# First attention of a two-layer block: max subtraction as four 32x64 products, preparation in 32-column strips with the keys one step ahead, reciprocals widened on GpSimd

## The chip, the core and the metric

One core of a Trainium2 chip. The metric is the device time of one execution in microseconds. The profiler records one execution; its span runs from the first to the last instruction, and the device time has a part outside it. PE is TensorE (matmuls; its weight loads are shown apart as PEld), DVE is VectorE, ACT is ScalarE, POOL is GpSimd, SP is SyncE.

## The reference

An input x of 128 sequences x 64 tokens x 128 channels goes through two layers, each a cross attention to a context (128 x 64 x 96) and a mixture of experts, each added to x with a tanh gate. The change touches the first attention alone:

```
xn = (x - mean(x)) / sqrt(var(x) + 1e-5)
q = xn @ wq + bq ; k = ctx @ wk + bk ; v = ctx @ wv + bv        # 16 heads of 8 channels
attn = softmax(q k^T / sqrt(8))                                 # per head, 64 x 64
x = x + tanh(g_xattn[0]) * ((attn v) @ wo + bo)
```

The rest (a mixture of 6 experts, the second attention with one head of 128, a mixture of 8 experts of which each token uses two) follows, and its code is not changed.

## The kernel before

x is held on chip as 64 tiles of 128 tokens (two sequences each). Four tiles make a group; there are 16 groups. The first attention is a software pipeline of steps: step t works on tile t for the scores, t-1 for the exponential, t-2 for the sums and the transposes of the probabilities, t-3 for the product with the values and t-4 for the output product. Within a group the steps are u0 to u3 (`u % GT`). The loop body holds eight steps, two groups. Every engine runs its own list of work in order, written out by hand in its `step`; semaphores join the lists. No planner sets the order.

On PE, a step runs: scores (L663, 32 rows x 64 columns of the array, with the head's keys spread so that four heads share one product), the subtraction of the row maxima from scores already in PSUM (L673, a product of the transposed maxima with a 0/1 matrix of head columns, added to the bank), in u0 the keys' preparation for the next group (L638), the output product (L686), the first half of the transposed probabilities (L690), the transpose of the widened reciprocals (L706), the product with the values (L719, 128 x 32 tiles), the preparation listed for the step in `PREP_AT` (u0: transposed rows L633, u1: queries L638, u2: values L644, u3: none), the second half of the transposes (L690), and the transpose of the maxima (L737).

ACT takes the exponential (L571), copies each PSUM bank out (L578 probabilities, L591 raw heads, L602 maxima, L542/L547/L554/L561 preparation), and normalises the rows of the group after next (L534, one tile in u1, one in u2, two in u3).

DVE makes the sums (L409), the maxima (L412), the reciprocals of the sums (L418), the maxima in two bf16 parts (L423, L425), the reciprocals widened from 16 heads to 128 channels (L430), the addition to x (L436), the product of raw heads and transposed reciprocals (L443), in u0 the layer norm's statistics of the group after next (L375, L379), in u1 its offset (L385), in u2 half the copy of the values (L393).

POOL's work has three parts per group. In u0 it makes the inverse deviation of the group after next (L70, L72) from DVE's statistics. In u1 it spreads the next group's keys into four zero-padded copies, one per head of a set of four (L494), and then adds the output bias to the group after next's x (L485), which waits for ACT's last normalisation of those rows, at the end of u3. In u2 and u3 it has nothing of its own.

PSUM has one bank for all four preparations (`prep`), so each waits for the copies of the one before. SP loads x and the context of a group once the values of the group two before are prepared. Two buffers alternate for scores, probabilities, spread keys and widened reciprocals; the narrow reciprocals have one.

Of the kernel before, what the change touches and what calls it, by code (L numbers as in the profile page):

```python
# [44 lines left out]
def static(t):  # L45
    return isinstance(t, int)
# [233 lines left out]
def attention_of_layer0(nc, sb, psum, sem, c, a, X, dispatch):  # L280
# [21 lines left out]
    denom = sb("a_denom", [P, H], F32)  # L302
    rec = sb("a_rec", [P, H], F32)
    wide_rec = [sb(f"a_wide_rec{i}", [P, H, DH], F32) for i in range(2)]
# [25 lines left out]
    KEYS, ROWS, QUERIES, VALUES = range(PREP)  # L330
    PREP_AT = ((ROWS,), (QUERIES,), (VALUES,), ())
    NORMALISE_AT = ((), (0,), (1,), (2, 3))
    LAST = TILES + 4

# [13 lines left out]
    def group_at(g0, more):  # L348

        return None if static(g0) and g0 + more >= G else g0 + more  # L350

    with nc.Block() as block:
# [16 lines left out]
        def _(dve):  # L369
# [26 lines left out]
            def step(t, u, g0):  # L396
# [17 lines left out]
                if m is not None:  # L414
                    dve.wait_ge(sum_done, m + 1)
                    if not static(m) or m >= 1:
                        dve.wait_ge(wide_rec_ready, m)
                    dve.reciprocal(rec[:], denom[:]).then_inc(rec_done, 1)  # L418
                if n is not None:
# [5 lines left out]
                    dve.tensor_tensor(max_parts[:, :, 1], max_by_bank, max_parts[:, :, 0], ALU.subtract).then_inc(parts_ready, 1)  # L425
                if m is not None:
                    if not static(m) or m >= 2:
                        dve.wait_ge(spread_mm, m - 1)
                    dve.wait_ge(rec_done, m + 1)
                    dve.tensor_copy(wide_rec[u % 2][:], rec[:].unsqueeze(2).broadcast_to([P, H, DH])).then_inc(wide_rec_ready, 1)  # L430
                w = tile_now(t, 4)
# [43 lines left out]
        @block.gpsimd  # L475
        def _(pool):
            def deviation(g):

                wait_alone(pool, stats_done, g + 1)
                inverse_deviation(pool, stats[:], c.minus_half[:], rstd[:], rstd_step, g)  # L480

            def add_bias(g):

                wait_alone(pool, xn_ready, g + 1)
                pool.tensor_tensor(X[:, bass.ts(g, GT), :], X[:, bass.ts(g, GT), :],  # L485
                                   c.out_bias0[:].unsqueeze(1).broadcast_to([P, GT, D]), ALU.add).then_inc(bias_added, 1)

            def spread_k(g, par):

                wait_alone(pool, prep_ev, PREP * g + KEYS + 1)  # L490
                if not static(g) or g >= 2:
                    wait_alone(pool, scores_mm, GT * (g - 1))
                for j in range(4):
                    last = pool.tensor_scalar(keys_of_head(par, j), kT[:],  # L494
                                              c.head_of_group[:, j:j + 1], None, ALU.mult)
                last.then_inc(k_heads_ready, 1)

            def step(t, u, g0):
                if u % GT == 0:
                    g = group_at(g0, 2)  # L500
                    if g is not None:
                        deviation(g)
                if u % GT == 1:
                    g = group_at(g0, 1)
                    if g is not None:
                        spread_k(g, (u // GT + 1) % 2)
                    g = group_at(g0, 2)
                    if g is not None:
                        add_bias(g)

            pool.memset(c.parts[:], 0.0)
            pool.memset(c.minus_half[:], -0.5).then_inc(c.zeroed, 1)
            pool.memset(c.v_heads[0][:].rearrange("p b u w -> p (b u w)"), 0.0).then_inc(c.zeroed, 1)
            wait_alone(pool, c.zeroed, 1)
            deviation(0)
            pool.memset(c.v_heads[1][:].rearrange("p b u w -> p (b u w)"), 0.0).then_inc(c.zeroed, 1)
            deviation(1)
            wait_alone(pool, c.out_bias_done, 1)
            add_bias(0)
            add_bias(1)  # L520
            loop_steps(pool, 2 * GT, TILES // (2 * GT) - 2, LAST, step)
            later_zeros(pool, c, dispatch)
            c.ln.deviation(pool, 0)
            c.ln.offset(pool, 0)

        @block.scalar
        def _(act):
# [36 lines left out]
            def step(t, u, g0):  # L564
# [15 lines left out]

                g = group_at(g0, 1)
                if u % GT == 0 and g is not None:
                    evacuate(g, (u // GT + 1) % 2, KEYS)
                if tile_now(t, 2) is not None:
                    keep_transposed(t - 2, 0)
                n = tile_now(t, 3)
                if n is not None:
# [3 lines left out]
                    act.copy(heads_raw[:], pv[:, 0]).then_inc(raw_ready, 1)  # L591
                g = group_at(g0, 1)
                if g is not None:
                    for k in PREP_AT[u % GT]:
                        evacuate(g, (u // GT + 1) % 2, k)
                if tile_now(t, 2) is not None:
# [25 lines left out]
        def _(pe):  # L622
            def prepare(g, par, k):
# [10 lines left out]
                if k in (KEYS, QUERIES):  # L634
                    w, src = (c.wk0, ctxT[par]) if k == KEYS else (c.wq0, xnT)
                    for h in range(2):
                        for odd in range(2):
                            last = pe.matmul(prep[S * odd:S * odd + S, bass.ts(h, GW // 2)], w[:, bass.ts(h, D // 2)],  # L638
                                             src[:].rearrange("p (t b q) -> p b t q", b=2, q=S)[:, odd],
                                             start=True, stop=True)  # L640
                if k == VALUES:
                    for b in range(GB):
                        for odd in range(2):
                            last = pe.matmul(prep[S * odd:S * odd + S, bass.ts(b, D // 2)], ctxT[par][:, bass.ts(b, S)],  # L644
                                             c.wv0[:].rearrange("p (u h w) -> p h u w", h=2, w=DH)[:, odd],
                                             start=True, stop=True)
                last.then_inc(prep_mm, 1)

            def step(t, u, g0):
# [19 lines left out]
                if n is not None:  # L669

                    pe.wait_ge(rows_ready, n + 1)
                    for s in range(2):
                        last = pe.matmul(scores[(u + 1) % 2][:, s, :], rows[bass.ts(s, STRIP), :], c.head_cols[bass.ts(s, STRIP), :],  # L673
                                         start=False, stop=True, skip_group_check=True)
                    last.then_inc(sub_mm, 1)
                g = group_at(g0, 1)
                if u % GT == 0 and g is not None:
                    prepare(g, (u // GT + 1) % 2, KEYS)
                n = tile_now(t, 4)
# [21 lines left out]
                if n is not None:  # L701
# [20 lines left out]
                    last.then_inc(pv_mm, 1)  # L722
                g = group_at(g0, 1)
                if g is not None:
                    for k in PREP_AT[u % GT]:
                        prepare(g, (u // GT + 1) % 2, k)
                n = tile_now(t, 2)
# [1287 lines left out]
```

## Time and profile before

| | |
|---|---|
| median of three runs | 916.31 us (911.5 to 917.06) |
| profiled execution | span 826.4 us; no total of its own is recorded |
| the runs' median less that span | 89.9 us |
| PE busy, share of the span | 91% |
| PEld | 71% |
| DVE | 83% |
| ACT | 69% |
| POOL | 57% |
| mean granted TensorE clock | 0.972 of full speed |

Busy shares are averages over the whole span, and the stages have different limits; the first attention fills the span from about 20 to 320 us. A matmul's busy time counts it from issue to a modelled end, and matmuls overlap, so a busy PE is not PE at its peak. In a timeline, several instructions of one line stand together as one row with their count, and the time in brackets is the idle time of that engine before the row, with what ended it. "Issue" there is time in which the engine waited for nothing that the profile shows.

### The profile page before, as it was taken

The page shows a single profiled execution, that of the slowest core. Times are in us where ns is not written, and L with a number is a line of the kernel's source. Part 1 is how long each engine was busy: PE and PEld are TensorE (multiplying, and loading weights), DVE is VectorE, ACT ScalarE, POOL GpSimd, SP SyncE. Part 2 cuts the span into 40 slices and gives each one's busy share as a digit, 9 for nine tenths or more (in the row PEclk, how much of TensorE's full clock was granted, in tenths as well). Part 3 has the DMA queues.
Part 4 walks back from the last instruction along what each step waited for, and adds up shares of the span by engine and source line. Part 5 has one row for each costly group of instructions (what it writes and reads, how often), then busy time and mean ns, then how long its engine had stood idle before and what let it go on. Part 6 is the DMA issues. An engine that isn't in the chain of part 4 may idle for free. (4 is left out here: it accounts for less than half of the span.)

```text
span 826.4 us, 26460 instructions
## 1 busy us (share of the span) xinstructions
PE 755.1 (91%) x8408; PEld 584.3 (71%) x8408; DVE 687.7 (83%) x2993; ACT 571.1 (69%) x1209; POOL 472.0 (57%) x504
## 2 busy tenths in 40 slices
PE   3899999999999997999999999998799999999970
PEld 2566666666666654667767767766699999999960
DVE  3889898988989896878888888977589888889965
ACT  2777777777777765688888898855566666666630
POOL 3445554444455601225777777776577777777770
PEclk9999999999999997999999999989999999999995
DMA  9200001000000002001111111113233443346838
GB/s 241 64 25 26 23 22 42 25 22 22 22 22 22 2 2 66 1 11 33 49 44 54 50 43 56 48 51 94 56 84 99 113 110 101 100 124 201 232 99 305
DMA packets 62212, 57.96 MB, mean 70 GB/s; under 512 B 10320, under 2 KB 52099, under 8 KB 62115
## 3 DMA queue, kind: packets, MB, share of 16 engines
q1 hardware_dynamic: 44547, 34.25, 15.3%
q0 software_dynamic: 8640, 17.84, 6.3%
q10 hardware_dynamic: 8928, 4.70, 2.0%
q8 instruction: 45, 0.74, 0.4%
q14 instruction: 52, 0.43, 0.2%
HBM read 32.74 MB, written 24.02 MB: 69 GB/s over the span
## 5 line engine op out<-in xcount | busy, mean ns | idle before, releaser
L1131 POOL DMA_INDIRECT contributions<-v_heads,d_token x142 | 141.6, 997 | 43.3 <-issue 25.3
L1115 POOL DMA_INDIRECT sorted_rows<-r_send,r_slots x128 | 126.5, 988 | 44.7 <-issue 42.0
L1860 PE MATMUL bc_bank<-d_xT,d_w 128*128 128x128 f32 x1136 | 151.7, 277 | 0.1
L1860 PEld LDWEIGHTS bc_bank<-d_xT,d_w 128*128 128x128 f32 x1136 | 139.0, 193 | 0.5 <-DVE d_xT L1377 0.4
L1636 ACT ACTIVATE b_hidden<-bc_bank 128x256 f32<-128x256 f32 x142 | 54.5, 384 | 72.5 <-PE bc_bank L1860 71.9
L494 POOL TENSOR_SCALAR a_k_heads<-a_kT,first 128x512 f32<-128x512 f32 x60 | 93.1, 1570 | 0.8 <-ACT a_kT L547 0.8
L1630 ACT COPY d_w<-w 128x512 f32 x142 | 87.1, 614 | 8.1 <-issue 6.0
L571 ACT ACTIVATE a_probs<-a_scores 128x1024 f32<-128x1024 f32 x64 | 65.6, 1025 | 29.4 <-PE a_scores L673 29.3
L412 DVE TENSOR_REDUCE a_neg_max<-a_scores 128x16 f32<-128x1024 f32 x64 | 78.1, 1221 | 8.1 <-PE a_scores L663 6.5
L578 ACT COPY a_probsT<-a_probsT_bank 128x512 f32<-128x512 f32 x128 | 74.8, 584 | 13.7 <-PE a_probsT_bank L690 13.2
L690 PE MATMUL a_probsT_bank<-first,a_probs 128*128 128x128 f32 x512 | 80.2, 279 | 2.2 <-ACT a_probsT L578 0.3
L409 DVE TENSOR_REDUCE a_denom<-a_probs 128x16 f32<-128x1024 f32 x64 | 77.3, 1209 | 1.7 <-issue 1.3
L663 PE MATMUL a_scores<-a_k_heads,a_qT 32*64 32x256 f32 x1024 | 70.8, 391 | 2.9 <-issue 2.8
L485 POOL TENSOR_TENSOR X<-X,out_bias 128x512 f32 (+1 forms) x16 | 20.3, 1271 | 87.5 <-ACT a_xn L534 84.9
L690 PEld LDWEIGHTS a_probsT_bank<-first,a_probs 128*128 128x128 f32 x512 | 57.9, 142 | 12.5 <-issue 6.0
L1705 PE MATMUL bc_bank<-b_xnT,w 128*128 128x512 f32 x96 | 50.2, 636 | 0.1
L1388 DVE TENSOR_SCALAR v_heads<-bc_bank,d_ends 128x128 f32<-128x128 f32 x142 | 48.7, 343 | 0.5 <-PE bc_bank L1879 0.5
L1756 PE MATMUL bc_bank<-w,b_weighted 128*128 128x128 f32 x384 | 46.8, 278 | 0.0
L663 PEld LDWEIGHTS a_scores<-a_k_heads,a_qT 32*64 32x64 f32 x1024 | 33.1, 132 | 19.3 <-issue 9.3
L1879 PE MATMUL bc_bank<-w_in,b_hidden 128*128 128x128 f32 x288 | 44.7, 278 | 0.5 <-DVE v_heads L1388 0.5
L1372 DVE TENSOR_TENSOR b_hidden<-b_hidden,bc_bank 128x256 f32<-128x256 f32 x72 | 30.1, 418 | 17.8 <-PE bc_bank L1879 10.5
L1756 PEld LDWEIGHTS bc_bank<-w,b_weighted 128*128 128x128 f32 x384 | 44.1, 192 | 0.4
(212 smaller groups left out, 1870.1 us busy)
## 6 DMA issues: line engine op xcount, KB each, us to landing
d_rows<-sorted_rows SPq DMA_DIRECT2D x142, 65.0 KB
X<-in_x SPq DMA_DIRECT2D x16, 256.0 KB, 3.0
b_hidden<-contributions SPq DMA_DIRECT2D x8, 512.0 KB
b_weighted<-contributions SPq DMA_DIRECT2D x8, 512.0 KB, 5.8
out_x<-X ACTq DMA_DIRECT2D x16, 256.0 KB
ctxT<-in_ctx_T SPq DMA_DIRECT2D x16, 192.0 KB, 2.9
c_ctxT<-in_ctx_T SPq DMA_DIRECT2D x16, 192.0 KB, 2.4
contributions<-v_heads,d_token POOLq DMA_INDIRECT x142
```

Source lines behind the costliest of these rows:

```text
L409: dve.reduce_sum(denom[:], probs[u % 2][:].rearrange("p (h k) -> p h k", k=S), AX_X).then_inc(sum_done, 1)
L412: dve.tensor_reduce(neg_max[:], scores[u % 2][:].rearrange("p a (h k) -> p (a h) k", k=S), AX_X, ALU.max, negate=True).then_inc(max_done, 1)
L494: last = pool.tensor_scalar(keys_of_head(par, j), kT[:], c.head_of_group[:, j:j + 1], None, ALU.mult)
L571: act.activation(probs[(u + 1) % 2][:], scores[(u + 1) % 2][:].rearrange("p a n -> p (a n)"), ACT.Exp, scale=SCALE0).then_inc(exp_done, 1)
L578: act.copy(probsT[u % 2][:, half * HU // 2:(half + 1) * HU // 2, :].rearrange("p u q -> p (u q)"), probsT_bank[:]).then_inc(pT_ev, 1)
L663: last = pe.matmul(scores[u % 2][S * b:S * b + S, s, bass.ts(h, 4 * S)], qT[par][rows_in, h, tile, :], k_heads[par][rows_in, tile, h].rear ...
L690: last = pe.transpose(probsT_bank[:, bass.ts(k, P)], probs[u % 2][:, bass.ts(half * HU // 2 + k, P)], c.ident[:])
L1115: pool.indirect_dma_start(dispatch.rows, bass.IndirectOffsetOnAxis(ap=slots[n % 2][:, k, j:j + 1], axis=0), send[n % 2][k][:, j, :], None) ...
L1131: pool.indirect_dma_start(dispatch.contributions, bass.IndirectOffsetOnAxis(ap=token[:, t % KEEP:t % KEEP + 1], axis=0), shares[t % KEEP], ...
L1630: act.copy(w12[t % 3][:], c.w12[:, bass.ds(experts[t % 4], 1)].rearrange("d a i h -> d (a i h)")).then_inc(w12_ready, 1)
L1756: last = pe.matmul(y[:, bass.ts(j, P)], weighted[n % 2][:, k, bass.ts(j, P)], c.w2_0[:, k, :], start=(k == 0), stop=(k == C0 - 1))
L1860: last = pe.matmul(uv[m % 2][:, bass.ts(i, P)], w12[m % 3][:, bass.ts(i, P)], xT[m % 4][:], start=True, stop=True)
```

## The change

The change has four parts, all in the first attention.

- The subtraction of the maxima (L673) is written as four products of 32 rows x 64 columns, one for each bank and half of the tokens, where it was two of 32 x 128.
- Keys, queries and values are prepared by products of 32 weight columns (128 x 32 tiles, the shape of L719) where they were of 64; there are twice as many products on as many streamed columns each.
- The keys' preparation and its copies by ACT move from u0 to u3 of the group before (PE: after the product with the values; ACT: after the raw heads), so the keys of a group are prepared one step earlier. The keys of group 1 are done in step 0.
- The widening of the reciprocals moves from DVE to POOL, first in POOL's step, for tile t-3; the narrow reciprocals get a second buffer. POOL's spreading of keys is divided over the steps (head 0 in u0 after the deviation, heads 1 and 2 in u1, head 3 in u2), the bias addition moves from u1 to u3, and the zero-filling for later stages from after the loop into step 62.

```diff
@@ -300,7 +300,7 @@
...
     denom = sb("a_denom", [P, H], F32)
-    rec = sb("a_rec", [P, H], F32)
+    rec = [sb(f"a_rec{i}", [P, H], F32) for i in range(2)]
     wide_rec = [sb(f"a_wide_rec{i}", [P, H, DH], F32) for i in range(2)]
@@ -328,8 +328,9 @@
...
     KEYS, ROWS, QUERIES, VALUES = range(PREP)
-    PREP_AT = ((ROWS,), (QUERIES,), (VALUES,), ())
+    PREP_AT = ((ROWS,), (QUERIES,), (VALUES,), (KEYS,))
     NORMALISE_AT = ((), (0,), (1,), (2, 3))
+    SPREAD_AT = ((0,), (1, 2), (3,), ())
     LAST = TILES + 4
@@ -348,6 +349,12 @@
...
         return None if static(g0) and g0 + more >= G else g0 + more
+    def preparations(t, u, g0):
+        first = [(1, KEYS)] if static(t) and t == 0 else []
+        parts = first + [(2 if k == KEYS else 1, k) for k in PREP_AT[u % GT]]
+        return [(group_at(g0, more), (u // GT + more) % 2, k) for more, k in parts if group_at(g0, more) is not None]
@@ -413,9 +420,9 @@
...
                     dve.wait_ge(sum_done, m + 1)
-                    if not static(m) or m >= 1:
-                        dve.wait_ge(wide_rec_ready, m)
-                    dve.reciprocal(rec[:], denom[:]).then_inc(rec_done, 1)
+                    if not static(m) or m >= 2:
+                        dve.wait_ge(wide_rec_ready, m - 1)
+                    dve.reciprocal(rec[u % 2][:], denom[:]).then_inc(rec_done, 1)
                 if n is not None:
@@ -423,11 +430,6 @@
...
                     dve.tensor_tensor(max_parts[:, :, 1], max_by_bank, max_parts[:, :, 0], ALU.subtract).then_inc(parts_ready, 1)
-                if m is not None:
-                    if not static(m) or m >= 2:
-                        dve.wait_ge(spread_mm, m - 1)
-                    dve.wait_ge(rec_done, m + 1)
-                    dve.tensor_copy(wide_rec[u % 2][:], rec[:].unsqueeze(2).broadcast_to([P, H, DH])).then_inc(wide_rec_ready, 1)
                 w = tile_now(t, 4)
@@ -485,25 +487,39 @@
...
-            def spread_k(g, par):
-                wait_alone(pool, prep_ev, PREP * g + KEYS + 1)
-                if not static(g) or g >= 2:
-                    wait_alone(pool, scores_mm, GT * (g - 1))
-                for j in range(4):
+            def spread_k(g, par, heads):
+                if heads[0] == 0:
+                    wait_alone(pool, prep_ev, PREP * g + KEYS + 1)
+                    if not static(g) or g >= 2:
+                        wait_alone(pool, scores_mm, GT * (g - 1))
+                for j in heads:
                     last = pool.tensor_scalar(keys_of_head(par, j), kT[:],
                                               c.head_of_group[:, j:j + 1], None, ALU.mult)
-                last.then_inc(k_heads_ready, 1)
+                if heads[-1] == 3:
+                    last.then_inc(k_heads_ready, 1)
+            def widen(n, par):
+                wait_alone(pool, rec_done, n + 1)
+                if not static(n) or n >= 2:
+                    wait_alone(pool, spread_mm, n - 1)
+                pool.tensor_copy(wide_rec[par][:], rec[par][:].unsqueeze(2).broadcast_to([P, H, DH])).then_inc(wide_rec_ready, 1)
             def step(t, u, g0):
+                n = tile_now(t, 3)
+                if n is not None:
+                    widen(n, (u + 1) % 2)
+                if static(t) and t == TILES - 2:
+                    later_zeros(pool, c, dispatch)
                 if u % GT == 0:
...
                         deviation(g)
-                if u % GT == 1:
-                    g = group_at(g0, 1)
-                    if g is not None:
-                        spread_k(g, (u // GT + 1) % 2)
+                g = group_at(g0, 1)
+                if g is not None and SPREAD_AT[u % GT]:
+                    spread_k(g, (u // GT + 1) % 2, SPREAD_AT[u % GT])
+                if u % GT == 3:
                     g = group_at(g0, 2)
@@ -519,7 +535,6 @@
...
             loop_steps(pool, 2 * GT, TILES // (2 * GT) - 2, LAST, step)
-            later_zeros(pool, c, dispatch)
             c.ln.deviation(pool, 0)
@@ -578,9 +593,6 @@
...
-                g = group_at(g0, 1)
-                if u % GT == 0 and g is not None:
-                    evacuate(g, (u // GT + 1) % 2, KEYS)
                 if tile_now(t, 2) is not None:
@@ -589,10 +601,8 @@
...
                     act.copy(heads_raw[:], pv[:, 0]).then_inc(raw_ready, 1)
-                g = group_at(g0, 1)
-                if g is not None:
-                    for k in PREP_AT[u % GT]:
-                        evacuate(g, (u // GT + 1) % 2, k)
+                for g, par, k in preparations(t, u, g0):
+                    evacuate(g, par, k)
                 if tile_now(t, 2) is not None:
@@ -634,14 +644,16 @@
...
                     for h in range(2):
-                        for odd in range(2):
-                            last = pe.matmul(prep[S * odd:S * odd + S, bass.ts(h, GW // 2)], w[:, bass.ts(h, D // 2)],
+                        for strip in range(4):
+                            odd, s = strip // 2, strip % 2
+                            last = pe.matmul(prep[bass.ts(strip, STRIP), bass.ts(h, GW // 2)], w[:, bass.ts(2 * h + s, STRIP)],
                                              src[:].rearrange("p (t b q) -> p b t q", b=2, q=S)[:, odd],
...
                     for b in range(GB):
-                        for odd in range(2):
-                            last = pe.matmul(prep[S * odd:S * odd + S, bass.ts(b, D // 2)], ctxT[par][:, bass.ts(b, S)],
+                        for strip in range(4):
+                            odd, s = strip // 2, strip % 2
+                            last = pe.matmul(prep[bass.ts(strip, STRIP), bass.ts(b, D // 2)], ctxT[par][:, bass.ts(2 * b + s, STRIP)],
                                              c.wv0[:].rearrange("p (u h w) -> p h u w", h=2, w=DH)[:, odd],
@@ -670,12 +682,10 @@
...
                     for s in range(2):
-                        last = pe.matmul(scores[(u + 1) % 2][:, s, :], rows[bass.ts(s, STRIP), :], c.head_cols[bass.ts(s, STRIP), :],
-                                         start=False, stop=True, skip_group_check=True)
+                        for b in range(2):
+                            last = pe.matmul(scores[(u + 1) % 2][bass.ts(b, S), s, :], rows[bass.ts(s, STRIP), bass.ts(b, S)],
+                                             c.head_cols[bass.ts(s, STRIP), :], start=False, stop=True, skip_group_check=True)
                     last.then_inc(sub_mm, 1)
-                g = group_at(g0, 1)
-                if u % GT == 0 and g is not None:
-                    prepare(g, (u // GT + 1) % 2, KEYS)
                 n = tile_now(t, 4)
@@ -720,10 +730,8 @@
...
                     last.then_inc(pv_mm, 1)
-                g = group_at(g0, 1)
-                if g is not None:
-                    for k in PREP_AT[u % GT]:
-                        prepare(g, (u // GT + 1) % 2, k)
+                for g, par, k in preparations(t, u, g0):
+                    prepare(g, par, k)
                 n = tile_now(t, 2)
...
                     pe.wait_ge(pT_ev, 2 * n + 1)

```

## Rows read from the trace of the kernel before

**Rows 1.** Busy time by stretch: length, PE, PEld, DVE, ACT, POOL, clock, DMA, GB/s.

```profile
133.14:151.39 18.25, 18.05 (x302) 11.99 (x300) 16.77 (x45) 14.20 (x32) 8.75 (x7) 1.00 0.08 25
...
151.39:169.96 18.57, 17.96 (x303) 12.01 (x301) 16.14 (x44) 14.20 (x32) 8.72 (x7) 1.00 0.08 25
```

**Rows 2.** Who waited for whom, whole span: total us, times, longest.

```profile
POOL X L485 <- ACT a_xn L534: 84.9, 15, 6.3
...
POOL a_rstd L70 <- DVE a_stats L379: 55.7, 16, 4.8
...
PEld a_scores L673 <- ACT a_rows L602: 21.4, 54, 1.0
```

**Rows 3.** Instructions by line: count, busy us, mean ns, idle time before.

```profile
L430 DVE COPY a_wide_rec<-a_rec 128x128 f32<-128x128 f32 x64 | 19.1, 299 | 0.6 <-DVE a_rec L418 0.5
...
L494 POOL TENSOR_SCALAR a_k_heads<-a_kT,first 128x512 f32<-128x512 f32 x60 | 93.1, 1570 | 0.8 <-ACT a_kT L547 0.8
...
L1102 POOL COPY r_send<-places 128x4 f32<-128x4 f32 x32 | 5.4, 200 | 0.1
```

**Rows 4.** Timeline, u1 into u2: start us, duration us, engine, line, tiles, count.

```profile
153.39 0.14 PEld L706 LDWEIGHTS a_pv<-first,a_wide_rec 128*128 128x128 f32 x1
...
155.30 0.42 PEld L690 LDWEIGHTS a_probsT_bank<-first,a_probs 128*128 128x128 f32 x4 [0.38 <-issue]
...
155.94 0.64 PEld L663 LDWEIGHTS a_scores<-a_k_heads,a_qT 32*64 32x64 f32 x16
...
156.61 0.26 ACT L602 COPY a_rows<-a_small 64x128 bf16<-64x128 bf16 x1
...
156.77 0.50 ACT L534 ACTIVATE a_xn<-X,a_minus_mean,a_rstd 128x128 f32 x1
...
156.97 0.39 PE L673 MATMUL a_scores<-head_cols,a_rows 32*128 32x512 bf16 x2
...
157.94 0.14 PEld L706 LDWEIGHTS a_pv<-first,a_wide_rec 128*128 128x128 f32 x1
```

**Rows 5.** Timeline, u3 into u0, PE's loads, ACT's normalisation and POOL.

```profile
144.45 0.14 PEld L706 LDWEIGHTS a_pv<-first,a_wide_rec 128*128 128x128 f32 x1
...
145.54 0.42 PEld L690 LDWEIGHTS a_probsT_bank<-first,a_probs 128*128 128x128 f32 x4 [0.30 <-ACT a_probsT L578]
...
146.88 0.88 ACT L534 ACTIVATE a_xn<-X,a_minus_mean,a_rstd 128x128 f32 x2
...
147.75 0.63 PEld L638 LDWEIGHTS a_prep<-ctxT,wkv 96*64 96x64 f32 x8 [0.23 <-issue]
...
148.09 1.27 POOL L485 TENSOR_TENSOR X<-X,out_bias 128x512 f32 x1 [6.01 <-ACT a_xn L534]
...
148.76 0.30 PEld L686 LDWEIGHTS a_small<-wo,a_heads_outT 128*128 128x128 f32 x2 [0.39 <-issue]
```

**Rows 6.** Timeline, from L706 in u0 to POOL's power L72.

```profile
149.42 0.14 PEld L706 LDWEIGHTS a_pv<-first,a_wide_rec 128*128 128x128 f32 x1
...
151.04 0.87 DVE L375 BATCH_NORM_STATS2 a_stats<-X 128x6 f32 x4
...
152.93 1.04 POOL L72 TENSOR_TENSOR a_rstd<-a_rstd,minus_half 128x4 f32<-128x4 f32 x1
```

**Rows 7.** Timeline, PE's loads for the values' preparation and for PV.

```profile
140.72 1.01 PEld L644 LDWEIGHTS a_prep<-wkv,ctxT 96*64 96x64 f32 x32
...
149.73 0.49 PEld L719 LDWEIGHTS a_pv<-a_probsT,v_heads 128*32 128x32 f32 x32 [0.17 <-issue]
```

**Rows 8.** Timeline of PE in the tail of the stage.

```profile
311.39 0.66 PE L690 MATMUL a_probsT_bank<-first,a_probs 128*128 128x128 f32 x4
...
314.84 0.49 PE L686 MATMUL a_small<-wo,a_heads_outT 128*128 128x128 f32 x2 [2.79 <-DVE a_heads_outT L443]
...
316.75 1.12 PE L690 MATMUL a_probsT_bank<-first,a_probs 128*128 128x128 f32 x4
```

**Rows 9.** The busy time by stretch, the tail of the stage.

```profile
315.00:320.00 5.00, 4.55 (x78) 3.57 (x78) 2.19 (x7) 1.81 (x5) 0.00 (x0) 0.66 0.00 2
```


## The prediction

> **What bounds the kernel now.** I read the busy time by stretch first, over two groups of four tiles in the middle of the first attention, cut where PE starts the scores of a group's second tile [rows 1]. A group takes 18.25 or 18.57 us (18.41 on average), and PE has matmuls in flight for 18 us of it, at the full granted clock. DVE is busy 16 to 17 us, ACT 14, POOL under 9. So PE sets the pace of this stage, with DVE close behind, and POOL is the only engine with room. That average hides where POOL's room lies, so I read the waits next [rows 2]: POOL sits 84.9 us in front of the bias addition (L485), waiting for the last normalised tile from ACT (L534), and 55.7 us in front of L70, waiting for DVE's statistics (L379). Today that costs nothing, for what stands behind these waits in POOL's order, the spread keys, is needed only several steps later. The change puts behind each of them something that PE needs at once. The rest of the reading is timelines, to see how late.
>
> Call the four steps of a group u0 to u3, and T0 the start of PE's scores (L663) in u0.
>
> **Part 1, the widening on POOL.** In step t POOL first widens tile t-3's reciprocals, which DVE made in step t-1. PE's L706 of the same step t transposes that tile and waits for it. POOL works in order, so the widening of u0 stands behind u3's bias addition, and that of u1 behind u0's deviation and one spread head. Nothing else waits long: u2 and u3 follow spread heads alone.
>
> *Wait A, PE's L706 in u0.* The bias addition waits for ACT's last two normalisations of u3. With KEYS now prepared and copied out in u3, that step has the shape that u1 has today with QUERIES [rows 4]: the next scores start at 155.94, ACT's normalisation at 156.77. Two tiles take 0.88 [rows 5], so the last ends at 157.65, which is T0+1.71. POOL starts 0.33 after it (146.88+0.88 to 148.09) and the addition takes 1.27 [rows 5]. Then comes the widening, an operation that POOL doesn't do today. Its nearest rows are a copy of 4 elements in 0.20 and a product of 512 in 1.57 [rows 3]; a straight line between them gives 0.53 for 128 elements. A plain copy should lie under a product with a strided output, so I take 0.40 and keep 0.20 and 0.53 as ends. With 0.10 to be seen by PE: T0 + 1.71 + 0.33 + 1.27 + 0.40 + 0.10 = T0+3.81. Unhindered, L706 comes 2.00 after the scores (155.94 to 157.94) [rows 4]. Wait A is 1.8 us.
>
> *Wait B, PE's L706 in u1.* From L706 in u0 the chain runs through PV, ACT's raw copy and DVE's product to the statistics of the group after next: 149.42 to 151.04, and on to POOL's power L72, which ends at 152.93+1.04=153.97 [rows 6]. That is 4.55 after L706. Then one spread head (1.57) [rows 3], the widening 0.40, and 0.10: 6.62. Today the two L706 lie 3.97 apart (149.42 [rows 6] to 153.39 [rows 4]). Wait B is 2.65 us.
>
> The bias addition with two groups' lead happens in 14 groups. B needs an older tile to widen, which the first group lacks, so 13. Together 14 x 1.8 + 13 x 2.65 = 59.7 us. With B over, POOL needs 3.14 for heads 1 and 2 and 0.40 to widen, against a step of 4.55 (151.39 [rows 1] to 155.94 [rows 4]), so u2 isn't held; head 3 and u3 need less.
>
> DVE's reciprocal gets a wait in turn, for the widening one step back; PE's L706 has waited for the same one by then, and behind the reciprocal on DVE stand only the maxima for scores that come later still: 0. The zero-filling for later stages moves in between the widenings of tiles 59 and 60, in a step in which POOL has no heads left, and the next widening is due a step later: 0.
>
> What leaves DVE is 19.1 us over 64 copies [rows 3]. While PE paces, and still more while it waits for POOL, DVE has that time free, so I count 0; were DVE the pace, the gain would reach 19.
>
> **Part 2, KEYS one step ahead.** In u0 PE loses the stretch 147.75 to 148.76 [rows 5], 1.01 us. In u3 it gains what a preparation adds between L706 and the second half of the transposes: 1.91 with QUERIES (153.39 to 155.30) [rows 4] less 1.09 without (144.45 to 145.54) [rows 5], 0.82. ACT's two copies of the keys move along and are in wait A. Net -0.19 in 15 groups: -2.9. The load of the context is asked for two groups ahead and its queue isn't passed; SP issues nothing more.
>
> **Part 3, strips of 32 columns.** Preparation then has PV's tile shape, so a change of shape between the two goes; the one after it stays (the 0.38 before L690 at 155.30 [rows 4]). Per preparation the gain lies between 0 and that 0.38; I take 0.1, nearer to nothing since what follows PV starts soon already: 45 x 0.1 = -4.5. VALUES goes from 32 loads in 1.01 to 64, at PV's rate (32 in 0.49) 0.98 [rows 7]: 0, at most +0.98 if each kept today's time.
>
> **Part 4, four 32x64 products.** Today's pair goes side by side in 0.39, and starts 0.10 after ACT's copy of the rows ends (156.61+0.26 to 156.97) [rows 4]. So it can come at most 0.1 sooner; if the four go two by two it costs 0.39 more. I count 0, as they are as many columns on as much of the array. In u0 and u1 the waits swallow either.
>
> **The sum.** Every second group is 0.32 longer today [rows 1], a pause at the loop's turn ahead of T0, while A is set by ACT and POOL; I let it be swallowed in 7: -2.2. So 59.7 - 2.9 - 4.5 - 2.2 = +50 us. The profiled execution has a span of 826.4 and no total of its own; the median of the runs, 916.3, leaves 89.9 around it, which the change doesn't touch. Span 876, time **966 us**.
>
> **Rivals.**
> *The clock falls in the waits.* In the tail of this stage PE waited 2.79 us before 314.84; soon after, the same four transposes took 1.12 where they had taken 0.66 [rows 8], and the stretch shows 0.66 granted [rows 9], a mix of 2.4 and 1.2 GHz. Wait B is nearly as long. A fall costs 0.46 on such a line; some three lines in a row make 1.4 us, and 13 of them +18: 984 us. Against it: within a group PE works without pause up to the wait, which the tail didn't. The Trainium skill, TensorE: Matmul & The Clock Gate, "Why this matters for your kernels", warns that idle gaps between bursts bring back the half-rate clock; the trace's tail agrees.
>
> *Faster: the shape changes are the whole story.* PE's idle time before L673 adds up to 21.4 us [rows 2]. Were that the cost of a changed shape and no wait for the rows, the four products would end it, and with parts 2 and 3 the time would be 916 - 21 - 7 = 888. It decides if the widening reaches PE within 2.0 of the scores in u0 and 3.97 after the last one in u1; POOL's chain alone (0.33 + 1.27 + 0.40 after ACT) is past the first. The Trainium skill, TensorEngine Tiling, "Key Properties", says that changing the tiling mode drains the array; the 0.38 at a change of shape agrees, and by that rule alone this rival would hold.
>
> *Less than the sum.* DVE is nearly the pace today. If half of its relief, the half that falls in u2 and u3, turns into time (-9.5), the strips give 0.38 each (-13) and the widening takes 0.20 (-5), the sum is +22: 938 us. For it: DVE is busy 16.8 of 18.25 us [rows 1]; against it: A and B are POOL's and ACT's, and a shorter PE step only lengthens the wait behind it.
>
> *The two sides cancel.* Gains of 21 (L673's idle time) and 19 us (DVE's copies) would have to meet waits of 40, two thirds of those worked out: 916 us. Nothing in the rows points there.
>
> **Chances and range.** My forecast 0.69, clock 0.18, less than the sum 0.07, cancelled 0.02, faster 0.04. A run here can tell 1% (9 us) from nothing: faster 0.04, same 0.02, slower 0.94. The bounds of the forecast: the widening's ends move 27 waits by -5 and +4; the strips by -13 and +5 (VALUES by +15); the four products in u2 and u3 by -3 and +12. Added, this is about 945 to 990; the case of less than the sum takes it to 940 and the clock to 992.
>
> **What would show it.** PE's L706 has an idle time in front of it, in u0 and u1 alone, 1.8 and 2.65 us, released by POOL's new copy; that copy starts at the end of L485 in u0 and of a spread head in u1. A group takes about 22 us, PE's share there falls to near 80%, and DVE and ACT wait more. The granted clock in the stage tells the first rival. A group of 18 us or less with no wait at L706 would prove me wrong, a widening of much over 0.53 or under 0.20 would mis-size both waits alike.

## The result, and the profile after

The changed kernel takes 956.63 us (median of four runs, 955.13 to 958.02) against 913.9 us in runs beside it: a ratio of 1.0478, with a 95% interval of 1.045 to 1.0506. The forecast was 966, slower, with a range of 940 to 992. Its profiled execution took 957.24 us with a span of 955.4. Ratios here and below compare fast executions; one slow one of the kernel before (3806.52 us) and the slow ones of the two filled kernels are left out of them.

The two waits are where the prediction put them. First the changed kernel's wait list, which answers to [rows 2]; L487 is now the bias addition, L507 POOL's widening, L716 PE's transpose of the reciprocals, L686 the maxima's products:

```profile
POOL X L487 <- ACT a_xn L549: 109.0, 15, 7.8
...
PEld a_pv L716 <- POOL a_wide_rec L507: 54.4, 27, 2.7
...
POOL a_rstd L70 <- DVE a_stats L386: 52.2, 16, 4.6
...
PEld a_scores L686 <- ACT a_rows L612: 15.9, 54, 1.0
```

PE waits 27 times for the widening, 54.4 us in all; before, L706 never waited. The rows of POOL's timeline for one u0 and u1, changed kernel, show what each copy stood behind:

```profile
151.24 1.26 POOL L487 TENSOR_TENSOR X<-X,out_bias 128x512 f32 x1 [7.67 <-ACT a_xn L549]
152.44 0.29 POOL L507 COPY a_wide_rec<-a_rec 128x128 f32<-128x128 f32 x1
156.02 0.23 POOL L70 TENSOR_SCALAR a_rstd<-a_stats 128x4 f32<-128x4 f32 x1 [3.29 <-DVE a_stats L386]
156.39 1.04 POOL L72 TENSOR_TENSOR a_rstd<-a_rstd,minus_half 128x4 f32<-128x4 f32 x1
157.42 1.58 POOL L497 TENSOR_SCALAR a_k_heads<-a_kT,first 128x512 f32<-128x512 f32 x1
158.94 0.29 POOL L507 COPY a_wide_rec<-a_rec 128x128 f32<-128x128 f32 x1
```

and the same stretch of PE's loads:

```profile
149.34 0.64 PEld L675 LDWEIGHTS a_scores<-a_k_heads,a_qT 32*64 32x64 f32 x16 [0.25 <-issue]
...
152.78 0.14 PEld L716 LDWEIGHTS a_pv<-first,a_wide_rec 128*128 128x128 f32 x1 [1.50 <-POOL a_wide_rec L507]
...
154.71 0.64 PEld L675 LDWEIGHTS a_scores<-a_k_heads,a_qT 32*64 32x64 f32 x16 [0.16 <-issue]
...
159.29 0.14 PEld L716 LDWEIGHTS a_pv<-first,a_wide_rec 128*128 128x128 f32 x1 [2.66 <-POOL a_wide_rec L507]
```

L716 starts within 0.1 us of the end of POOL's copy both times, 3.44 after T0 (149.34, the scores of u0) and 6.51 after the one before. The groups come in two lengths. The busy time by stretch of the changed kernel, cut at L716 of u1 (columns as in [rows 1]):

```profile
115.72:138.18 22.46, 18.92 (x356) 12.57 (x356) 16.39 (x39) 14.01 (x31) 9.70 (x12) 0.92 0.06 20
138.18:159.29 21.11, 17.38 (x357) 11.74 (x357) 16.48 (x39) 13.90 (x31) 9.71 (x12) 1.00 0.07 22
```

Both hold the same work and the same two waits. In the first, PE's granted clock was at half for a part of the group (116.7 to 120.1 us) (0.92 is a mix of 2.4 and 1.2 GHz), and it is 1.35 us longer. Of the twelve whole groups from 48 to 310 us, six took 22.4 to 22.6 us and six 21.1, where a group took 18.25 or 18.57 before [rows 1]. The stage's last product of raw heads and reciprocals starts at 365.5 us.

### The profile page after: what moved, and what is told of

Same layout as the page of the kernel before. It is cut to its first block and busy times, and to the rows that moved or that the text cites. A ratio compares the mean times of both kernels' runs of the same rounds, so it can differ in the third digit from the quotient of the medians.

```text
span 955.4 us, 28351 instructions
## 1 busy us (share of the span) xinstructions
PE 783.2 (82%) x9304; PEld 597.5 (63%) x9304; DVE 688.3 (72%) x2929; ACT 564.7 (59%) x1209; POOL 484.4 (51%) x568
## 5 line engine op out<-in xcount | busy, mean ns | idle before, releaser
L1139 POOL DMA_INDIRECT contributions<-v_heads,d_token x142 | 138.2, 973 | 104.6 <-PE bc_bank L1887 65.7
L1868 PE MATMUL bc_bank<-d_xT,d_w 128*128 128x128 f32 x1136 | 160.3, 285 | 36.4 <-DVE d_xT L1385 30.6
L700 PE MATMUL a_probsT_bank<-first,a_probs 128*128 128x128 f32 x512 | 82.5, 285 | 0.3
L487 POOL TENSOR_TENSOR X<-X,out_bias 128x512 f32 (+1 forms) x16 | 20.2, 1264 | 111.7 <-ACT a_xn L549 109.0
L675 PE MATMUL a_scores<-a_k_heads,a_qT 32*64 32x256 f32 x1024 | 75.2, 411 | 0.1
L716 PE MATMUL a_pv<-first,a_wide_rec 128*128 128x128 f32 x64 | 19.4, 303 | 48.0 <-POOL a_wide_rec L507 48.0
L1380 DVE TENSOR_TENSOR b_weighted<-b_hidden,bc_bank 128x256 f32<-128x256 f32 x70 | 29.0, 414 | 36.6 <-PE bc_bank L1887 21.1
L445 DVE TENSOR_TENSOR a_heads_outT<-a_heads_raw,a_pv 128x128 f32<-128x128 f32 x64 | 18.3, 285 | 46.1 <-ACT a_heads_raw L603 42.1
L1878 PE MATMUL bc_bank<-first,d_rows 128*128 128x128 f32 x142 | 39.7, 280 | 13.9 <-DVE d_xT L1385 10.0
L603 ACT COPY a_heads_raw<-a_pv 128x128 f32<-128x128 f32 x64 | 17.0, 266 | 55.8 <-PE a_pv L729 55.0
```

The costliest lines, as they stand in the source:

```text
L675: last = pe.matmul(scores[u % 2][S * b:S * b + S, s, bass.ts(h, 4 * S)], qT[par][rows_in, h, tile, :], k_heads[par][rows_in, tile, h].rear ...
L700: last = pe.transpose(probsT_bank[:, bass.ts(k, P)], probs[u % 2][:, bass.ts(half * HU // 2 + k, P)], c.ident[:])
L1139: pool.indirect_dma_start(dispatch.contributions, bass.IndirectOffsetOnAxis(ap=token[:, t % KEEP:t % KEEP + 1], axis=0), shares[t % KEEP], ...
L1380: dve.tensor_tensor(d_hidden[m % 4].rearrange("p k n -> p (k n)"), silu[m % 2], uv[m % 2][:, KH * P:2 * KH * P], ALU.mult).then_inc(h_read ...
L1868: last = pe.matmul(uv[m % 2][:, bass.ts(i, P)], w12[m % 3][:, bass.ts(i, P)], xT[m % 4][:], start=True, stop=True)
```

## The experiments

Each kernel ran beside the kernel before, whose runs, but for that one, lay between 908 and 926 us; ratios are to those. "Per group" is the distance between two transposes of the reciprocals in u1 (L716 in the changed kernel, another line number in others), read from each trace in mid-stage.

**The kernel before, once more.**

> The kernel before, unchanged, profiled once more. The profile of the changed kernel lies 129 us above that of before (955.4 against 826.4 us of span) where the timed runs differ by 43, and its own execution took only 1.8 us more than its span. If the part of 89.9 us that the prediction put around the span is real, this profile has a span of about 826 and a time of about 916. If instead the first profile of before caught an execution whose later stages went faster, the time lies within 2 us of the span, the span is near 910, the first attention ends near 320 us as before, and the 85 us stand in the last stage, after 570 us.

Measured: span 919.2, time 921.01. The first attention has the same groups (18.25 and 18.57) and ends at 319.5 us instead of 320.0. Most of the difference stands in the last stage, as ACT's copies of expert weights show by their first and last start, here in the first profile of before:

```profile
L1630 ACT COPY d_w<-w x142: 602/611/634, 577.2 to 794.1; 128x512 f32 x142
```

and in the second:

```profile
L1630 ACT COPY d_w<-w x142: 603/612/632, 601.7 to 886.5; 128x512 f32 x142
```

216.9 us against 284.8 for the same 142 copies; another 24.5 us stand between the first attention and the first of them. So the first profile caught an execution with faster later stages; there are 1.8 us around a span, not 89.9. The stage that the change touches is alike in both.

**The widening back on DVE.**

```diff
+                if m is not None:
+                    if not static(m) or m >= 2:
+                        dve.wait_ge(spread_mm, m - 1)
+                    dve.wait_ge(rec_done, m + 1)
+                    dve.tensor_copy(wide_rec[u % 2][:], rec[u % 2][:]...).then_inc(wide_rec_ready, 1)
                 w = tile_now(t, 4)
...
             def step(t, u, g0):
-                n = tile_now(t, 3)
-                if n is not None:
-                    widen(n, (u + 1) % 2)
```

> The changed kernel with the widening of the reciprocals back on DVE; POOL's split spreading and late bias addition stay. Theory 1 (position: the widening stands behind two blocked waits in POOL's order, 27 waits of 54.4 us in all, and the clock falls in them): no wait before the transpose of the reciprocals, no clock fall between 40 and 320 us, 890 to 905 us. Theory 2 (the reshaped products or the moved keys cost the time): stays above 930. Theory 3 (POOL is the wrong engine whatever the order, by its own speed or by sharing with DVE): also 890 to 905, so it's the next kernel that tells theory 3 from theory 1.

Measured: 911.03 us, ratio 0.9928 (0.9905 to 0.9951). 17.61 and 17.77 us per group, no wait for the reciprocals, the clock at full from the first groups to the tail of the stage (304.9 us). On a base of 914 that is 907 us, just over the forecast of 890 to 905, but far from the 930 of theory 2. The other three parts are a gain; the loss is the widening's.

**POOL widens one step earlier.**

```diff
-                n = tile_now(t, 3)
+                n = tile_now(t, 2)
                 if n is not None:
-                    widen(n, (u + 1) % 2)
+                    widen(n, u % 2)
```

> The changed kernel with POOL widening the reciprocals in the step in which DVE makes them (tile t-2 in place of t-3), so that each copy stands ahead of the deviation and of the bias addition. Theory 1 (position): both waits of PE go, the granted clock stays at full, 885 to 905 us, up to 10 below the version with the widening on DVE since DVE loses 19 us of copies. Theory 3 (POOL as an engine): 940 or more.

Measured: 905.07 us, ratio 0.9836 (0.9811 to 0.9861), faster than both kernels. One group of it:

```profile
129.53:146.83 17.30, 17.21 (x359) 11.78 (x358) 15.84 (x40) 13.80 (x32) 9.84 (x12) 1.00 0.08 27
```

and its rows of POOL at the turn from u3 to u0:

```profile
139.72 0.29 POOL L507 COPY a_wide_rec<-a_rec 128x128 f32<-128x128 f32 x1 [2.55 <-DVE a_rec L425]
142.83 1.28 POOL L487 TENSOR_TENSOR X<-X,out_bias 128x512 f32 x1 [2.82 <-ACT a_xn L549]
```

The copy now stands ahead of the blocked bias addition. The same 64 copies at the same 0.29 us on the same engine, one step earlier in its order, are worth 6.1% of the time (1.0478 to 0.9836). POOL as an engine (theory 3) is out.

**The widening on POOL alone.** PE and ACT as before, `PREP_AT` with an empty last entry, the keys in u0, old shapes; DVE and POOL as in the change.

> The kernel before with only the widening on POOL and POOL's new order (split spreading, bias addition in u3); preparation, its place and the maxima's products as before. Theory 1 (position): both waits are there, about 914 + 54 + 9 (clock) less little = 965 to 980 us, more than the whole change. Theory 2 (reshaped products): 905 to 920.

Measured: 968.52 us, ratio 1.0555 (1.0523 to 1.0586). Only the wait in u1 is there, 2.41 to 2.55 us; the one in u0 is 0.2 or nothing, since the keys' preparation ahead of the transpose (here L721) fills it:

```profile
167.22 0.63 PEld L653 LDWEIGHTS a_prep<-ctxT,wkv 96*64 96x64 f32 x8 [0.23 <-issue]
...
169.15 0.14 PEld L721 LDWEIGHTS a_pv<-first,a_wide_rec 128*128 128x128 f32 x1 [0.23 <-POOL a_wide_rec L507]
...
175.51 0.18 PEld L721 LDWEIGHTS a_pv<-first,a_wide_rec 128*128 128x128 f32 x1 [2.41 <-POOL a_wide_rec L507]
```

In place of the second wait the clock fell in 9 of the 11 groups from 67 to 312 us, so the forecast of the time came true with one of its two waits missing. The reshaped products (theory 2) are out.

**One copy moved, ahead of the bias addition.**

```diff
-                if n is not None:
+                if n is not None and u % GT != 0:
                     widen(n, (u + 1) % 2)
+                n = tile_now(t, 2)
+                if n is not None and u % GT == 3:
+                    widen(n, u % 2)
```

> The changed kernel with one copy moved: in u3 POOL widens the reciprocals of the next step's tile too, ahead of the bias addition, so that the copy PE needs in u0 no longer stands behind it; the one of u1 stays behind the deviation. Theory 1 (each wait is the position of one copy, and the two add): the wait in u0 (14 of 1.50 us) goes, the one in u1 (13 of 2.5 to 2.66) stays as long as it is, some clock falls go with it: 930 to 937 us. Rival (POOL's chain is one length and the wait only changes its place): the wait in u1 grows to about 4 us and the time stays at 950 or more.

Measured: 945.23 us, ratio 1.0342 (1.03 to 1.0383), or 945 on a base of 914: a gain of 12 us, not 20 to 27. The wait in u0 is gone and the one in u1 is 2.69 to 2.80, so the rival (4 us) falls too. A group without a fall takes 20.0 us, 1.1 less than 21.1. Two things were missed, of about 5 us each. The group shrank by 1.1 us where a wait of 1.50 went. And the clock fell in eight of the twelve groups, in two of them for twice the time.

**The other copy moved, ahead of the deviation.** The same edit with `u % GT != 1` and `u % GT == 0`.

> The changed kernel with the other copy moved: in u0 POOL widens the next step's tile too, ahead of the deviation, so the copy PE needs in u1 doesn't stand behind it; the one of u0 stays behind the bias addition. If the two waits add: 14 waits of 1.50 us remain, the 13 of 2.6 go (34 us), groups of 18.5 us; if only the long wait lets the clock fall, no falls, 914 to 920 us. If a wait of 1.5 is enough for falls: 922 to 928.

Measured: 936.5 us, ratio 1.0175 (1.0145 to 1.0206), which is 930 on a base of 914, over my 914 to 928. The wait in u1 went, and a new one came in u2, as its loads show:

```profile
147.94 0.14 PEld L719 LDWEIGHTS a_pv<-first,a_wide_rec 128*128 128x128 f32 x1 [1.26 <-POOL a_wide_rec L507]
...
158.19 0.14 PEld L719 LDWEIGHTS a_pv<-first,a_wide_rec 128*128 128x128 f32 x1 [1.50 <-POOL a_wide_rec L507]
```

Between the deviation and the copy for u2 POOL now spreads three heads in a row:

```profile
141.96 1.04 POOL L72 TENSOR_TENSOR a_rstd<-a_rstd,minus_half 128x4 f32<-128x4 f32 x1
142.99 4.65 POOL L497 TENSOR_SCALAR a_k_heads<-a_kT,first 128x512 f32<-128x512 f32 x3
147.59 0.29 POOL L507 COPY a_wide_rec<-a_rec 128x128 f32<-128x128 f32 x1
```

I had taken u2 as safe because wait B had made PE late enough. A group takes 19.65 or 19.84 us and the clock stays at full in all of them: here waits of 1.26 and 1.50 didn't let it fall; one of 2.4 to 2.8 did in most groups of the two kernels above.

**The waits filled with products nobody reads**, 10 and 20 of 128 columns.

> The changed kernel with products nobody reads put in front of PE's transpose of the reciprocals, 10 in u0 and 20 in u1, about 1.1 and 2.2 us, a little shorter than the waits of 1.5 and 2.6 us. If the clock's falls are a cost of their own (7 in the stage, groups with one 22.3 to 22.6 us against 21.0 to 21.2 without), the granted clock stays at full, the waits shrink to 0.4 each, and the time is 945 to 950 us. If the falls cost nothing on the path: 957 or more.

Measured: 1004.25 us, ratio 1.0889 (1.0836 to 1.0943). The size was wrong: for each f32 product written the trace holds two loads and two products, so the fill was 2.40 and 4.63 us, about twice as long as the waits, and groups took 23.8 us; four groups, those with a turn of PE's loop, took 30.3 to 31.1. No other group shows a fall, but at these lengths that doesn't price one. Again, shorter:

```diff
-                    pe.wait_ge(wide_rec_ready, n + 1)
                     if not static(n) or n >= 1:
                         pe.wait_ge(o_ready, n)
+                    if group_at(g0, 2) is not None and u % GT < 2:
+                        for _ in range(3 if u % GT == 0 else 5):
+                            pe.matmul(pv[:].rearrange("p a q -> p (a q)"), c.ident[:], c.first[:, 0:2 * P], ...)
+                    pe.wait_ge(wide_rec_ready, n + 1)
```

> The fill again, cut to size: products of 256 columns, 3 in u0 and 5 in u1, by the scores' columns (256 in 0.21 us, twice for f32) 1.3 and 2.1 us, both under the waits of 1.50 and 2.52 to 2.66. If a fall costs 1.36 us per group (22.45 against 21.10 us in the changed kernel), no fall is left between 40 and 330 us, every group takes 21.1 us, the stage is 8 to 9 us shorter and the time 947 to 950. If the falls go but the groups stay at 22.4, the falls weren't what made those groups longer.

Measured: 991.19 us, ratio 1.0726 (1.0674 to 1.0779), so the forecast of the time failed. The trace is of the longest of its four executions (996.16 us; the others took 980 to 993). Three groups of it, the third with the loop's turn:

```profile
90.56:111.68 21.12, 20.70 (x372) 14.55 (x373) 16.36 (x39) 13.96 (x31) 9.72 (x12) 1.00 0.08 23
111.68:132.78 21.10, 20.98 (x372) 14.59 (x373) 16.41 (x39) 13.90 (x31) 9.71 (x12) 1.00 0.07 22
132.78:162.23 29.45, 22.18 (x372) 15.38 (x373) 15.93 (x39) 14.14 (x31) 9.70 (x12) 0.88 0.06 18
```

The first four groups, which took 22.4 to 22.5 us with falls in the changed kernel, take 21.0 to 21.1 at full clock: within a group a fall costs the 1.36 us that the two lengths gave. The loss is elsewhere, in the turn of PE's loop, which takes two groups:

```profile
150.92 0.31 PEld L675 LDWEIGHTS a_scores<-a_k_heads,a_qT 32*64 32x64 f32 x8 [7.23 <-issue]
```

and the page's list of DMA queues tells what PE waited for, here this kernel:

```profile
q8 instruction: 84, 1.38, 0.6%
```

and the changed kernel, without the fill:

```profile
q8 instruction: 48, 0.79, 0.4%
```

At four turns PE stood still for 7.23, 8.31, 7.63 and 8.17 us, and these groups took 29.45 to 32.00 us, 38 us more together than at 21.1; the first turn, near 102 us, cost nothing of the kind. Of the 36 more packets of 16 KB, 34 lie between 102 and 340 us, where the changed kernel has none up to 320. As the fill's instructions are the only difference, the loop's body was fetched again.

**The parts alone, on the kernel before.** The strips, the four products, and the keys' move (with POOL's split spreading and late bias addition, which belong to it):

> The kernel before with only the 32-column strips in the preparation. The prediction took 0.1 us per preparation, -4.5 in all, for one change of array shape less; in the trace of the changed kernel the strips start 0.41 after the product with the values where the old ones started 0.58 after it, so 0.17 for two of the three moved ones before: about 914 to 919 against 919 here, first attention ending near 315. Rival (twice as many instructions cost more than a drain saves): 922 or more.

> The kernel before with only the four 32x64 products. The prediction counted 0 (-3 to +12). In the trace of the changed kernel the four follow the scores by 0.84 where ACT's copy of the rows was early (the old pair always followed by 1.02), so up to 0.18 us in each of 64 steps where the rows are early, nothing where they are late: 909 to 917 against 919 here. Rival (the four go two by two): 925 to 930.

> The kernel before with only the keys moved to u3 (with POOL's split spreading and late bias addition, which go with it); widening on DVE, old shapes. The prediction took -2.9 us. The version with the widening on DVE is 0.9928 of before, strips alone 1.0007, four products alone 0.995; if the parts add, this one is about 0.997, 3 us, with the first attention's groups near 18.2 us. If the new array shapes need each other and the keys' place (preparation next to the product of the same shape), this one shows 0 and the sum of the parts falls short of 0.9928.

Measured: strips 1.0007 (0.9984 to 1.0029), 18.07 and 18.40 us per group; four products 0.995 (0.9927 to 0.9973), 18.02 and 18.33; keys 0.9982 (0.9963 to 1.0), 18.15 and 18.25. Added they make 0.9939, beside 0.9928 for all three in one kernel; the parts add as far as the intervals tell. The time of the strips alone can't be told from none; per group they are 0.17 us shorter. Where the four products gain, one step of the kernel before shows,

```profile
137.83 0.64 PEld L663 LDWEIGHTS a_scores<-a_k_heads,a_qT 32*64 32x64 f32 x16
138.44 0.26 ACT L602 COPY a_rows<-a_small 64x128 bf16<-64x128 bf16 x1
138.85 0.09 PEld L673 LDWEIGHTS a_scores<-head_cols,a_rows 32*128 32x128 bf16 x2 [0.39 <-ACT a_rows L602]
```

beside the same step with the four products alone:

```profile
137.55 0.64 PEld L663 LDWEIGHTS a_scores<-a_k_heads,a_qT 32*64 32x64 f32 x16
138.06 0.26 ACT L602 COPY a_rows<-a_small 64x128 bf16<-64x128 bf16 x1
138.37 0.11 PEld L674 LDWEIGHTS a_scores<-head_cols,a_rows 32*64 32x64 bf16 x4 [0.18 <-ACT a_rows L602]
```

The pair comes 1.02 us after the scores in each of the steps from 133 to 152 us, though ACT's copy ended anywhere from 0.57 to 0.88 after them. The four come 0.05 behind the copy. So the profile's releaser is the last one it knows of: part of the 21.4 us of [rows 2] was no wait for ACT.

**The better version with the old shapes of preparation.**

> The version that widens one step earlier (0.9836 of before, 17.27 us per group), with the preparation's old 64-column shapes. With DVE relieved PE alone paces the stage, so a change of array shape should now cost what it takes: 0.17 us at two to three preparations of a group, 17.6 to 17.8 us per group, 0.988 to 0.992. If the strips are worth nothing even there: 0.9836 again.

Measured: 910.47 us, ratio 0.988 (0.986 to 0.9901), 17.65 us per group against 17.27 with strips. With DVE relieved the strips are worth 0.38 us per group, twice what they gave before. It is the step from the product with the values to a preparation, here in u1 without strips,

```profile
130.25 0.49 PEld L727 LDWEIGHTS a_pv<-a_probsT,v_heads 128*32 128x32 f32 x32 [0.17 <-issue]
130.83 0.63 PEld L648 LDWEIGHTS a_prep<-a_xnT,first 128*64 128x64 f32 x8
```

and with them, in the version that widens one step earlier:

```profile
129.84 0.49 PEld L729 LDWEIGHTS a_pv<-a_probsT,v_heads 128*32 128x32 f32 x32 [0.17 <-issue]
130.26 0.62 PEld L649 LDWEIGHTS a_prep<-a_xnT,first 128*32 128x32 f32 x16
```

That is 0.58 us against 0.42; it is 0.59 against 0.42 in u2 and 0.58 against 0.50 in u3.

## Why the prediction was right

**The cause, by steps.** The order on POOL was the cause, and both waits were priced from rows of before. *Wait A* was to be 1.8 us and is 1.40 to 1.51: the widening takes 0.29, not 0.40; ACT ends 0.07 sooner after T0, and POOL starts 0.07 sooner after ACT. *Wait B* was to be 2.65 and is 2.48 to 2.66; its chain is 6.35 or 6.51 long where I summed 6.62. 27 waits were counted and 27 are there, 54.4 us for 59.7. POOL's copy for u2 and u3 indeed waits for nothing long.

**The gains were sized too small.** The stage ends 46 us later than before (365.5 against 319.5), of which waits are 54.4 and the falls about 7 x 1.36 = 9.5, so the rest of the change gave back 18 us. I had 9.6 (-2.9, -4.5, -2.2). The three parts beside the widening gave 10 of the 18: with the widening on DVE the stage ends at 309.6. Among them the four products, counted at 0, gave 3 to 5 us alone (0.23 us per group, and 0.995), since I had bounded their gain by one step in which the copy of the rows ended late, 0.93 after the scores (155.94 to 156.87). The keys gave 1 to 2 us of the 2.9, the strips alone nothing clear of noise. The other 8 us of the 18 are what the long waits in u0 and u1 swallow of PE's other waits, the loop's pause among them (0.32 in five groups before, where I counted seven), and perhaps DVE's relief (next paragraph); no run parts these.

**DVE's relief.** I counted 0 for the 19.1 us of copies. With the waits gone it is worth what lies between 0.9928 and 0.9836, some 8 us (the stage ends at 302.4 in place of 309.6). The wait lists from 60 to 275 us show where, at the transpose of the maxima, first with the copies on DVE:

```profile
PE a_small L747 <- DVE X L443: 5.3, 18, 0.5
...
PEld a_small L747 <- DVE parts L432: 4.8, 8, 0.7
```

and then with POOL widening one step earlier:

```profile
PEld a_small L745 <- DVE parts L432: 1.8, 6, 0.3
```

The load and the product of one transpose stand in both of the first lines, so they don't add. In the kernel before (its second profile) the same stretch has no wait for DVE there: DVE came to hold PE only when the other three parts had made PE's steps shorter. Whether 0 was right in the change itself, where PE comes late by POOL, isn't shown.

**The clock rival came about on top of the forecast, not in its place.** I gave it 0.18, and held against it that PE works without pause up to the wait. It fell all the same in about half of the groups, at the price I had put on it (1.4, measured 1.36). So the mechanism and its two waits were right, and the total was right by some luck as well: forecast +50, measured +43, from 54.4 us of waits in place of 59.7, 18 us given back in place of 9.6, and 9.5 us of clock in place of nothing. The range was added up wrongly too: 966 + 4 + 5 + 15 + 12 is 1002, and about 990 only without the 15 of the values.

**What was wrong: "89.9 around it".** The span of 826.4 belonged to an execution whose later stages ran 83 to 96 us faster than in any other trace (506.4 us from the end of the first attention to the end of the span, against 599.7 in the second profile of before, 589.9 after and 589 to 603 in all), and the time around a span is 1.8 us. The forecast didn't suffer, since the change was added to the runs' median and the touched stage was the same in both. Why that one execution was faster there stays open.

The rival "faster" is refuted by the four products alone: 0.995, where it needed all of the 21.4 us. Its rule holds in the small: the four products have the scores' tile shape and are worth 0.23 us per group, the strips have that of the product with the values and are worth 0.17 to 0.38.

## What to carry to other kernels

An idle engine takes over work only at the place where it goes into the engine's order: read what that engine waits for, not how busy it is, and put the new work ahead of the waits. Here the same copy, one step earlier, turned 4.8% lost into 1.6% won. When a wait is taken out, look at what the next instruction of that queue delays (u2, after the deviation), and price a wait of two to three microseconds on PE with the clock's fall as well.

## What the runs showed of the hardware

The granted clock fell in single groups though PE was busy for 18.9 of 22.5 us in them. Waits of 1.26 and 1.50 us in a group never brought it down. One of 2.4 to 2.55 did in 9 of 11 groups in the widening on POOL alone, one of 2.69 to 2.80 in eight of twelve with the copy ahead of the bias addition. In the changed kernel, with 1.50 and 2.6, it fell in six of twelve with the same work, so that the same kernel has two kinds of groups.

POOL's addition of two inputs goes with a slower DVE instruction beside it: the cast of the maxima (L430) takes 0.69 to 0.79 us in all twelve places from 48 to 310 us of the changed kernel where L487 runs at the same time, and 0.17 elsewhere, beside POOL's spreading too.

What a turn of PE's loop costs depends on the length of its body. At 356 loads and as many products per group, two groups to the body, a turn left the instruction queue at 48 packets; at 372 each it took 84, and PE stood still for 7.23 to 8.31 us at four turns. The Trainium skill, Runtime: NRT & Kernel Launch, "Instruction fetch mechanics", says that a taken branch whose target isn't among the two pages held stops for a fetch by DMA. The fetch is seen here, but not that number: 34 packets of 16 KB over the four turns are eight or nine for a body, and the shorter body, 4% less, turned with none.
